# One load for the eight block numbers of a half step, in a graph and attention kernel

## The chip, the cores and the metric

The kernel runs on one core of one Trainium2 chip. The metric is the device time of one execution in microseconds (us). The kernel before has a median of 3451.71 us over three runs (3448.81 to 3453.6).

## The reference, cut to what matters

A node matrix x of 6250 rows by 256 goes through three branches. The first is a graph step: `support = xn @ weight`, then one message for each of 200,000 edges, summed by destination.

```python
support = x @ weight
msgs = edge_val[:, None] * support[edge_col]
agg = jax.ops.segment_sum(msgs, edge_row, num_segments=N_NODES)
return jax.nn.relu(agg + bias + x)
```

In the reference's call the rows that are gathered are numbered by dst and the rows that are summed into by src. The second branch is a linear attention layer with eight heads and a feed-forward layer (the mixer). The third, on the sum of the first two, is a mixture of eight experts with the best two chosen for each row. Only the graph step's sum is touched by the change.

## The kernel before

The kernel has three stages. First the edges are sorted by block of 128 summed rows, and `support` is written to memory. Then comes the gather stage. Then the expert stage follows.

In the gather stage the sorted edges lie in NG = 1624 groups of 128, each group for one block only. Eight groups (HALF = 8) are a half step, and there are STEPS_G = 203 half steps, all written out in the program. A group takes four stations:

- POOL (GpSimd) issues one indirect DMA at L766. It fetches 128 rows of `support` into `rows[h]`. There are ROWS = 4 such buffers, so the gather of half step s waits until the products of half step s - 4 are done (semaphore `summed`). POOL can thus be 32 groups ahead and no more.
- ACT builds the matrix `hot` at L1243 from `is_low`, which DVE makes at L1554 (`select`) three half steps ahead.
- PE multiplies `hot` by `rows` at L929 (`sum_half`), two groups to a unit, each unit in its own PSUM bank. A unit waits for its gathers, and for the adds of the same bank in the half step before (semaphore `carried`).
- DVE adds each product to the running sum of its block: R[block] += ps, L1567 in `carry_on`. These adds are called carries here. The block number is in `dest_i` in SBUF, so DVE's sequencer reads it into a register at L1561 (`value_load`), checks its bounds, works out the address and waits for the carry before and, once for each unit, for PE's products.

The order of work on DVE and PE is written out by hand. On DVE a half step s is `select(s + 3)`, `carry_on(s)`, a `convert` of the next window of edge records every eighth half step, and then pieces of the mixer. Until half step 41 these pieces are the keys and values of the attention. From half step BEGIN = 42 they are the groups of four blocks of the mixer, one group every EVERY = 12 half steps (`widen`, `queries`, `weigh_heads`, `layer_norm`, `add_halves`, `finish`). PE has its own pieces in the same half steps (L946 to L1003). So the carries of DVE, the products of PE and the pieces of the mixer wait for each other in one chain, beside POOL's gathers.

When the mixer's last group is done (`ff2_done`), SP loads the first rows and weights of the expert stage (`first_tail_loads`, L574 and L567), while the last gathers run. After the last carry, `finish(FULL, 1)` ends the stage, and SP and POOL wait for `carried` to reach NG.

In the rows, "DVEq" is DVE's sequencer. TENSOR_LOAD is the register load, the FUSED_REGOPS and the SEQ_ASSERT of L1561 are the bounds check of one number, and the FUSED_REGOPS of L1567 is the address, which also carries the wait for the carry before.

Of the kernel before, what the change touches and what calls it, by code (L numbers as in the profile page):

```python
# [13 lines left out]
ds = bass.ds  # L14
# [15 lines left out]
NB = -(-N // P)  # L30
# [28 lines left out]
HALF = 8  # L59
# [117 lines left out]
def program(nc, x, src, dst, edge_weight, gnn_w, gnn_b, Wq, bq, Wk, bk, Wv, bv, Wo, bo,  # L177
# [10 lines left out]
    with ctx:  # L188
# [3 lines left out]
        def alloc(stack, name, shape, dt=F32):  # L192
            return stack.enter_context(nc.sbuf_tensor(name, shape, dt))
# [85 lines left out]
        dest_i = alloc(early, "dest_i", [P, NG], I32)  # L279
# [27 lines left out]
        R = alloc(early, "R", [P, NB + 1, D])  # L307
# [1055 lines left out]
        def _(dve):  # L1363
# [191 lines left out]
                                  in1=t_low[a][:, None, col:col + HALF].to_broadcast([P, P, HALF]), op=ALU.is_equal).then_inc(is_low_done, 1)  # L1555

            def carry_on(s):
                for q in range(UNITS):
                    for t in range(2):
                        g = s * HALF + q * 2 + t  # L1560
                        where = dve.value_load(dest_i[0:1, g:g + 1], min_val=0, max_val=NB)  # L1561
                        there = R[:, ds(where, 1), :].rearrange("p a d -> p (a d)")
                        if g:
                            dve.wait_ge(carried, g)
                        if t == 0:
                            dve.wait_ge(summed, s * UNITS + q + 1)
                        dve.tensor_tensor(out=there, in0=there, in1=ps[q][:, t * D:(t + 1) * D], op=ALU.add).then_inc(carried, 1)  # L1567
# [113 lines left out]
            for s in range(STEPS_G):  # L1681
                if s + AHEAD_LOW < STEPS_G:
                    select(s + AHEAD_LOW)
                carry_on(s)
                if s % WIN == 1 and s // WIN + 1 < NWIN:
                    convert(s // WIN + 1)
# [285 lines left out]
```

## Time and profile before

| | |
|---|---|
| median of three runs | 3451.71 us |
| the profiled execution's own time | 3441.95 us |
| span of its trace | 3440.2 us |
| gather stage, first gather to last carry | 696.1 to 2813.7 us |
| granted clock of TensorE, mean over the span | 0.83 of full speed |

Every time of the rows is from this one execution. Its own time is 1.75 us above its span, and 9.8 us below the median. Busy time alone doesn't say which engine sets the end of a stage: register, branch and semaphore instructions aren't counted as busy, and POOL needs some time after each DMA before it begins the next.

### The profile page before, as it was taken

The page shows a single profiled execution, that of the slowest core. Times are in us where ns is not written, and L with a number is a line of the kernel's source. Part 1 is how long each engine was busy: PE and PEld are TensorE (multiplying, and loading weights), DVE is VectorE, ACT ScalarE, POOL GpSimd, SP SyncE. Part 2 cuts the span into 40 slices and gives each one's busy share as a digit, 9 for nine tenths or more (in the row PEclk, how much of TensorE's full clock was granted, in tenths as well). Part 3 has the DMA queues.
Part 4 walks back from the last instruction along what each step waited for, and adds up shares of the span by engine and source line. Part 5 has one row for each costly group of instructions (what it writes and reads, how often), then busy time and mean ns, then how long its engine had stood idle before and what let it go on. Part 6 is the DMA issues. An engine that isn't in the chain of part 4 may idle for free.

```text
span 3440.2 us, 46797 instructions
## 1 busy us (share of the span) xinstructions
PE 2606.8 (76%) x10870; PEld 1931.2 (56%) x10870; DVE 2346.8 (68%) x5310; ACT 1248.0 (36%) x2681; POOL 2226.2 (65%) x2110
## 2 busy tenths in 40 slices
PE   5888888667877786786786787787688754888886
PEld 2677777545544454564554565555555533776775
DVE  7999999745555656657656656656656657877863
ACT  0111111045444343344344343343344423444532
POOL 2355555577777777777777777777777733554552
PEclk9666666579889888988898998898898965999998
DMA  3111110065453543453554544445444386555445
GB/s 126 39 34 34 34 34 26 12 127 121 119 125 111 118 117 115 124 121 117 123 119 122 118 119 124 119 116 127 115 107 116 111 185 219 132 130 135 104 87 117
DMA packets 418876, 370.29 MB, mean 108 GB/s; under 512 B 248648, under 2 KB 357232, under 8 KB 418256
## 3 DMA queue, kind: packets, MB, share of 16 engines
q0 software_dynamic: 105424, 247.55, 28.0%
q1 hardware_dynamic: 304720, 110.37, 13.6%
q10 hardware_dynamic: 8496, 9.75, 0.8%
q8 instruction: 84, 1.38, 0.2%
q14 instruction: 152, 1.25, 0.1%
HBM read 299.09 MB, written 74.81 MB: 109 GB/s over the span
## 4 chain that ended last, share of the span: by engine, by line
PE 23%; DVE 20%; issue 12%; POOL 9%; DVEq 7%; DMA 6%; SPq 1%; ACT 1%; POOLq 0%; ACTq 0%
POOL rows L766 8%; DVE R L1567 8%; PE ps L929 6%; DVEq L1561 5%; PE ps L1003 5%; PE ps L995 4%; PE ps L1053 3%; DMA total<-y_w,zt 2%; DMA rows<-support,t_dst 2%; DVEq L1567 1%; DMA zt<-routed 1%; PE ps L963 1%; DVE xnT L1627 1%; DVE is_low L1554 1%; DVE stats L1482 1%
## 5 line engine op out<-in xcount | busy, mean ns | idle before, releaser
L766 POOL DMA_INDIRECT rows<-support,t_dst x1624 | 1598.5, 984 | 503.3 <-issue 462.7
L929 PE MATMUL ps<-rows,hot 128*128 128x256 f32 x3248 | 927.5, 435 | 377.9 <-DVE R L1567 259.8
L1567 DVE TENSOR_TENSOR R<-R,ps 128x256 f32 x1624 | 683.2, 421 | 754.3 <-DVE R L1567 474.8
L929 PEld LDWEIGHTS ps<-rows,hot 128*128 128x128 f32 x3248 | 669.8, 217 | 623.7 <-issue 383.4
L1243 ACT ACTIVATE hot<-is_low,t_w 128x128 f32<-128x128 bf16 x1624 | 689.4, 512 | 188.2 <-DVE is_low L1554 149.3
L740 POOL DMA_INDIRECT slots<-rec,st_pos x224 | 323.3, 1443 | 341.5 <-issue 194.9
L873 PE MATMUL ps<-spread,piece 128*104 128x96 bf16 x1568 | 306.2, 372 | 52.0 <-DVE spread L1476 51.8
L873 PEld LDWEIGHTS ps<-spread,piece 128*104 128x104 bf16 x1568 | 301.4, 286 | 63.8 <-DVE spread L1476 34.0
L810 POOL DMA_INDIRECT total<-y_w,zt x105 | 166.5, 1585 | 235.0 <-DMA total<-y_w,zt 177.2
L1053 PE MATMUL ps<-w_all,h_s 128*128 x1260 | 178.1, 291 | 37.2 <-DVE h_s L1894 36.3
L1053 PEld LDWEIGHTS ps<-w_all,h_s 128*128 128x128 f32 x1260 | 161.6, 192 | 63.9 <-issue 61.4
L1053 PE MATMUL ps<-w_all,z_s 128*128 x630 | 180.4, 423 | 10.3 <-issue 9.3
L1003 PE MATMUL ps<-w_sb,uT 128*128 128x256 f32 x784 | 173.3, 379 | 0.0
L995 PE MATMUL ps<-xnT,w_sb 128*128 128x512 f32 (+1 forms) x416 | 173.1, 568 | 0.0
L1003 PEld LDWEIGHTS ps<-w_sb,uT 128*128 128x128 f32 x784 | 149.0, 190 | 20.3
L789 POOL DMA_INDIRECT routed<-zx,pos_r x98 | 102.8, 1049 | 79.4 <-DVE pos_r L1813 50.5
L1554 DVE TENSOR_TENSOR is_low<-iota_x,t_low 128x1024 bf16<-128x1024 bf16 x203 | 137.8, 679 | 11.5 <-ACT hot L1243 10.0
L1341 ACT ACTIVATE h_act<-h_act 128x512 f32<-128x512 f32 x105 | 66.4, 632 | 215.5 <-DVE h_act L1902 215.5
L1053 PEld LDWEIGHTS ps<-w_all,z_s 128*128 128x128 f32 x630 | 115.5, 195 | 43.8 <-issue 23.6
L1160 ACT ACTIVATE xnT<-ps 128x512 f32<-128x512 f32 (+1 forms) x104 | 53.8, 569 | 219.0 <-PE ps L853 219.0
L1169 ACT ACTIVATE rec<-ps 104x384 bf16<-104x384 f32 x56 | 27.5, 491 | 283.4 <-PE ps L873 283.4
L946 PE MATMUL ps<-wkv_sb,xnT 128*128 128x512 f32 x196 | 107.4, 676 | 23.8 <-ACT h L1250 19.0
(261 smaller groups left out, 3350.5 us busy)
## 6 DMA issues: line engine op xcount, KB each, us to landing
rows<-support,t_dst POOLq DMA_INDIRECT x1624, 2.8
zt<-routed SPq DMA_DIRECT2D x105, 134.0 KB, 2.1
xa<-in_x SPq DMA_DIRECT2D x24, 512.0 KB
out<-total SPq DMA_DIRECT2D x1, 6250.0 KB, 21.7
xin<-in_x SPq DMA_DIRECT2D x12, 512.0 KB
support<-sup_sb ACTq DMA_DIRECT2D x12, 512.0 KB
xf<-in_x SPq DMA_DIRECT2D x12, 512.0 KB
xnb<-xb SPq DMA_DIRECT2D x12, 512.0 KB, 3.6
```

Of the source, the lines that this page charges most:

```text
L740: pool.indirect_dma_start(out=slots, out_offset=bass.IndirectOffsetOnAxis(ap=st_pos[k][0:KP, c:c + 1], axis=0), in_=rec[k][0:KP, c, :, :]. ...
L766: pool.indirect_dma_start(out=rows[h][:, j, :], out_offset=None, in_=support, in_offset=bass.IndirectOffsetOnAxis(ap=t_dst[a][:, col:col + ...
L810: pool.indirect_dma_start(out=total, out_offset=bass.IndirectOffsetOnAxis(ap=zt[i % RING][:, TOK:TOK + 1].bitcast(I32), axis=0), in_=y_w[i ...
L873: last = pe.matmul(ps[2 + half][0:KP, o:o + RUN * NF], lhsT=piece[:, j, :, c], rhs=spread[:, j, :, :, c], start=(j == 0), stop=(j == JT - 1))
L929: last = pe.matmul(ps[q][:, t * D:(t + 1) * D], lhsT=hot[o][:, q * 2 + t, :], rhs=rows[h][:, q * 2 + t, :], start=True, stop=True)
L995: last = pe.matmul(ps[4 + f % 2][:, 0:T], lhsT=w1_sb[:, c, f * P:(f + 1) * P], rhs=hT[:, c, 0:T], start=(c == 0), stop=(c == KC - 1))
L1003: last = pe.matmul(ps[6 + j // 2][:, (j % 2) * D:(j % 2 + 1) * D], lhsT=uT[:, f, j * P:(j + 1) * P], rhs=w2_sb[:, f, :], start=(f == 0), s ...
L1053: ins = pe.matmul(to, lhsT=a(s), rhs=b(m), start=(first and n == 0), stop=(last and n == 2))
L1243: last = act.activation(hot[o][:, k, :], is_low[h][:, :, k], ACT.Copy, scale=t_w[a][:, col:col + 1])
L1554: dve.tensor_tensor(out=is_low[h][:, :, :], in0=iota_x[:, :, :], in1=t_low[a][:, None, col:col + HALF].to_broadcast([P, P, HALF]), op=ALU. ...
L1561: where = dve.value_load(dest_i[0:1, g:g + 1], min_val=0, max_val=NB)
L1567: dve.tensor_tensor(out=there, in0=there, in1=ps[q][:, t * D:(t + 1) * D], op=ALU.add).then_inc(carried, 1)
```

## The change

The eight block numbers of a half step are loaded at the head of `carry_on` by one call that covers eight neighbouring columns of `dest_i`, into eight registers of DVE. The bounds given are the same. The adds then take their numbers from these registers. Nothing else is changed: the order of the adds, their waits and the other engines' programs stay.

```diff
             def carry_on(s):
+                _, where = nc.values_load_multi_w_load_instructions(dest_i[0:1, s * HALF:(s + 1) * HALF], [mybir.EngineType.DVE], min_val=0, max_val=NB)
                 for q in range(UNITS):
                     for t in range(2):
                         g = s * HALF + q * 2 + t
-                        where = dve.value_load(dest_i[0:1, g:g + 1], min_val=0, max_val=NB)
-                        there = R[:, ds(where, 1), :].rearrange("p a d -> p (a d)")
+                        there = R[:, ds(where[q * 2 + t], 1), :].rearrange("p a d -> p (a d)")
                         if g:
                             dve.wait_ge(carried, g)
                         if t == 0:
```

## Rows read from the trace of the kernel before

**Rows 1.** The page's part 1: busy us, share of the span, instructions.

```profile
PE 2606.8 (76%) x10870; PEld 1931.2 (56%) x10870; DVE 2346.8 (68%) x5310; ACT 1248.0 (36%) x2681; POOL 2226.2 (65%) x2110
```

**Rows 2.** Waits of POOL over the span: us in total, times, longest us.

```profile
POOL rows L766 <- issue: 462.7, 1519, 0.3
...
POOL rows L766 <- PE ps L929: 36.6, 104, 3.0
```

**Rows 3.** Gathers (L766) by stretch: stretch, its us, POOL busy (count), clock, DMA, GB/s.

```profile
0.00:1248.00 1248.00, 420.67 (x432) 0.74 0.30 77
...
0.00:2250.00 2250.00, 1186.90 (x1206) 0.80 0.38 96
...
0.00:2548.00 2548.00, 1411.10 (x1432) 0.81 0.39 99
...
0.00:2790.00 2790.00, 1595.55 (x1621) 0.82 0.40 101
```

**Rows 4.** Carries (L1567) by the same stretches: DVE busy (count).

```profile
0.00:1248.00 1248.00, 178.23 (x424) 0.74 0.30 77
...
0.00:2250.00 2250.00, 494.49 (x1176) 0.80 0.38 96
...
0.00:2548.00 2548.00, 588.93 (x1400) 0.81 0.39 99
...
0.00:2790.00 2790.00, 676.43 (x1608) 0.82 0.40 101
```

**Rows 5.** Timeline of POOL: start us, us, instruction, idle before it and its releaser.

```profile
2294.77 0.95 POOL L766 DMA_INDIRECT rows<-support,t_dst  x1 [0.84 <-PE ps L929]
...
2548.28 0.96 POOL L766 DMA_INDIRECT rows<-support,t_dst  x1 [3.00 <-PE ps L929]
```

**Rows 6.** Lines L1561, L1567, DVE's sequencer: ns min/median/max, first and last start.

```profile
L1561 DVEq TENSOR_LOAD <-dest_i x1624: 296/300/1521, 716.9 to 2812.6; - x181
L1561 DVEq FUSED_REGOPS  x1624: 190/190/207, 717.5 to 2812.9; - x181
L1561 DVEq SEQ_ASSERT  x1624: 23/23/39, 717.8 to 2813.1; - x181
...
L1567 DVEq FUSED_REGOPS  x1624: 57/57/57, 717.9 to 2813.2; - x181
```

**Rows 7.** Timeline of DVE in the mixer's part of the gather stage.

```profile
2166.41 0.42 DVE L1567 TENSOR_TENSOR R<-R,ps 128x256 f32 x1 [7.22 <-PE ps L929]
...
2178.40 0.97 DVE L1567 TENSOR_TENSOR R<-R,ps 128x256 f32 x2
...
2232.97 0.42 DVE L1567 TENSOR_TENSOR R<-R,ps 128x256 f32 x1
2233.73 0.42 DVE L1567 TENSOR_TENSOR R<-R,ps 128x256 f32 x1 [0.34 <-DVE R L1567]
2234.56 0.42 DVE L1567 TENSOR_TENSOR R<-R,ps 128x256 f32 x1 [0.41 <-DVE R L1567]
```

**Rows 8.** Line L1561, two short stretches: the first register load of two half steps.

```profile
L1561 DVEq TENSOR_LOAD <-dest_i x1: 309/309/309, 2176.6 to 2176.6; - x1
...
L1561 DVEq TENSOR_LOAD <-dest_i x1: 316/316/316, 2232.1 to 2232.1; - x1
```

**Rows 9.** Waits of DVE, then PE, from 2152 to 2280 us, twelve half steps.

```profile
DVE R L1567 <- PE ps L929: 17.2, 14, 7.2
...
PE ps L929 <- DVE R L1567: 18.7, 11, 5.8
```

**Rows 10.** The stage's end: SP's and PE's timelines; DMA issues, whole span, then 2782 to 2808 us.

```profile
2757.54 0.36 SPq L567 DMA_DIRECT2D work<-xnb  x1
...
2808.33 3.58 PE L929 MATMUL ps<-rows,hot 128*128 128x256 f32 x8 [1.26 <-DMA rows<-support,t_dst]
...
rows<-support,t_dst POOLq DMA_INDIRECT x1624, 2.8
...
rows<-support,t_dst POOLq DMA_INDIRECT x10, 16.0
```

## The prediction, made before the change was run

> **What bounds the kernel now.** I read the page first. PE is the busiest engine, DVE and POOL come behind it, and none is near full [rows 1], so busy shares don't name the bound. The gather stage takes 2118 of 3440 us, and the change lies wholly in it, so I asked each engine there what it waits for.
>
> POOL's answer decides. It issues 1624 gathers, and before 1519 of them its idle time is put down to nothing but issue, 462.7 us or 0.30 us each. The other 104 were released by PE, 36.6 us in all; taking 0.30 us off each of those as the same issue time leaves 5.4 us [rows 2]. So POOL stands truly still for about 5 us in the stage and otherwise issues without a pause. Three of those waits stick out; the first is 0.84 us at 2294, the last 3.00 us at 2548 [rows 5].
>
> Next I counted gathers and carries over the same stretches, which shows how far POOL is ahead of DVE. At 1248 us it is 432 - 424 = 8 groups, at 2250 us 1206 - 1176 = 30, at 2548 us 1432 - 1400 = 32, at 2790 us 1621 - 1608 = 13 [rows 3, 4]. The ring of four `rows` buffers allows 32. So the reader should see two chains. POOL needs 1002 / 774 = 1.295 us for a group between 1248 and 2250 us, the chain of PE, DVE and mixer pieces 1002 / 752 = 1.332 us [rows 3, 4]. For the 96 groups of twelve half steps that is 124.3 against 127.9 us. The chain is a little slower, eats the ring's slack for some nine mixer groups, and only then makes POOL wait. POOL sets the stage's length; the chain costs the 5 us at its end.
>
> **The change part by part.** Before, each carry costs DVE's sequencer one load of 0.300 us, a check of 0.190 and 0.023 us, and an address of 0.057 us [rows 6]. That is 0.57 us. Carries of one unit start 0.76 us apart [rows 7]: 2233.73 less 2232.97. So 0.76 - 0.57 = 0.19 us lie between four instructions, 0.047 us each. The first carry of a unit also waits for PE's semaphore; it comes 0.83 us after the one before (2234.56 less 2233.73), 0.07 us more. Eight carries span 4 x 0.76 + 3 x 0.83 = 5.5 us from the first start to the last, plus 0.85 us from the first load at 2232.1 to the first carry at 2232.97 [rows 7, 8].
>
> What sets this pace is the sequencer: a carry itself takes 0.42 us [rows 7], and DVE idles 0.34 to 0.41 us before the next. Where registers and wait were ready, two carries took 0.97 us together [rows 7], that is 0.55 us apart.
>
> - Removed: seven of eight loads per half step, 7 x 0.35 us of sequencer time. The checks stay, one for each number, since the bounds are still given; I see nothing that would merge them into less work.
> - Moved: all eight checks now stand ahead of the first carry. Load 0.30, checks 8 x (0.190 + 0.023) = 1.70, address 0.06, and 18 gaps of 0.047 = 0.85: 2.9 us from the load's start to the first carry, against 0.85 us. Behind it the carries follow at 0.55 us, a span of 7 x 0.55 = 3.9 us instead of 5.5 us. Sequencer-held half steps therefore take 2.9 + 3.9 = 6.8 us instead of 6.35: +0.45 us. The reason is that the seven removed loads and checks used to run partly under the 0.42 us of the carry ahead of them; the moved ones have no carry to hide under.
> - The price of a load of eight registers is not in this trace. From below it is 0.30 us, a load of one. From above it is eight loads, 8 x 0.35 = 2.8 us. I take about 0.3 us. The recorded load is mostly a trip to SBUF and back, since an instruction that stays in the sequencer takes 0.02 to 0.06 us [rows 6], and one instruction makes one trip.
>
> The Trainium skill speaks against the change here. "Perfetto Trace Analysis", section "DVE / Act Engine Instruction", says that the sequencer pushes an engine instruction into a wait queue and is then free to decode the next. By that rule work spread between carries is partly free, work in front of the first is not. The trace agrees: the load of the next number was over before the carry's 0.42 us were. Left to that rule alone, every half step would pay the 0.45 us.
>
> But a half step is not always held by the sequencer. I went through the twelve of one mixer group, 2149 to 2276 us, from the first register load of each to its first carry.
>
> - In four, DVE waits for PE's product, 7.22 us in the longest case [rows 7]; there the 2.9 us are hidden. All gain 1.6 us of span, but PE is then busy with its own mixer work, and only one of the four, at 2166 us, stands ahead of DVE work that PE needs: -1.6 us.
> - In five, the load starts while DVE still works off queued mixer pieces, so the first carry comes 1.8 to 3.8 us after it; 2176.6 to 2178.40 us is the shortest case [rows 7, 8]. Such a half step loses at most 2.9 - 1.8 = 1.1 us and gains 1.4 to 1.6 us of span: -0.3 us at least, -1.4 us at the longest cover, about -3 us for the five.
> - Three are like 2232.1 us, held by the sequencer: +0.45 us each. The last stands before a wait for PE and costs nothing, so +0.9 us.
>
> The sum is -3.7 us a group, 127.9 to about 124.2 us, level with POOL's 124.3. That this is DVE's to give shows in the waits: in those 126 us PE waits 18.7 us for carries, DVE 17.2 us for products [rows 9]. The ring's slack is then no longer eaten, and POOL's waits of 5 us go. POOL's own 0.98 us and 0.30 us per gather are untouched, and they hide all the rest. If that cover were gone the change would be worth 12 x 3.7 = 44 us.
>
> Before half step 42 the chain is faster than POOL, and 0.45 us more for a half step against a slack of 24 groups (32 - 8) delays nothing.
>
> **The end of the stage.** SP's first loads for the expert stage go out at 2757.54 us, when the mixer is done. From then the gathers land late: a median of 16.0 us after issue between 2782 and 2808 us against 2.8 us over the whole span, and the last products start at 2808.33 us, released by a gather's landing [rows 10]. With the chain no longer 13 to 32 groups behind, the mixer ends nearer to POOL's last gathers in order, so the loads begin about 5 us earlier against POOL's count, and four more gathers land in the slow stretch. From 2757.5 to 2808.3 us POOL's pace has room for 51 / 1.295 = 39 gathers, and the landing time grows by 13.2 us, 0.34 us a gather; four more make about +1.5 us. The last four carries lose 0.2 us each where PE doesn't hold them: -0.2 us. Behind the stage all is shifted alike.
>
> **The rivals.**
>
> - The front load is too dear (slower). If the load of eight costs far over 0.3 us, the half steps that are held by the sequencer, and those with a short cover, pay it, about 6.5 in a group. The gain of 3.7 us is gone at 2.9 + 3.7 / 6.5 = 3.5 us ahead of the first carry, a load of 0.87 us. As the ring's slack is used up today, each further us per group counts twelvefold, and +0.6 us a group makes the kernel slower by 7 us. At 0.1 us for each further register the load takes 1.0 us: +0.9 us a group, 11 us, 3463 us. If the call is only eight loads in a row, so that the change doesn't do what it says, the front is 5.2 us: 6.5 x 2.3 - 3.7 = +11 us a group, 130 us, 3580 us. For it speaks that the trace prices no such load; against it, the short times of all that stays in the sequencer.
> - Hidden anyway (same). If what makes POOL wait at 2294 to 2548 us is PE's mixer work and not the carries, the 5 us stay: 3451 us. PE is what released POOL [rows 5], but PE itself waits 18.7 us for carries in a group [rows 9].
> - The slow landings go too (faster). If the earlier expert loads are through before the last gathers, these land 2.8 us after issue instead of 16.0 us: 13 us on top of 5, about 3434 us. Against it: from 2782 to 2808 us the gathers alone were slow, long after the loads went out, and POOL kept adding to them.
>
> **How the numbers follow.** Sum for the forecast: -5.0 + 1.5 - 0.2 = -3.7 us. The profiled execution's own 3441.95 us would be 3438.3 us; the median of the runs lies 9.8 us above it, and from 3451.7 us I get 3448.0 us. A measurement of this kernel can tell about 0.2%, 7 us, from no change.
>
> Chances: forecast, -1 to -7 us, 0.50; hidden 0.13; dear front load 0.21, of it 0.04 for eight separate loads; landings too 0.16. The forecast and the hidden case are "same", with a little of each neighbour, 0.60; the landings and the forecast's far end are faster, 0.20; the dear load is slower, 0.20. The range reaches from near the landings' case, 3436 us, to a load of somewhat over 1 us, 3470 us: beyond lie some 0.08 below and 0.11 above.
>
> **What would show each step.** In the changed kernel 203 register loads stand where 1624 stood, each near 0.3 us, with eight checks behind it before the first address. First carry 2.9 us after a load's start in sequencer-held half steps; carries 0.55 us apart, not 0.76 and 0.83. POOL less than 25 groups ahead at 2250 us, and no wait over 0.3 us. Last gather issued near 2789 us. The prediction is wrong if the load is over 0.9 us, if the carries stay over 0.7 us apart, if checks are merged or dropped (then the chain is faster still, and the time the same, since POOL holds), or if the landings at the end move by over 5 us.

## The result, and the profile after

The changed kernel takes 3440.13 us, the median of seven runs (3437.51 to 3443.41), against 3451.71 us for the kernel before (seven runs, 3445.84 to 3456.54). The ratio is 0.9966, with a 95% interval of 0.9956 to 0.9976: 11.6 us faster. A later comparison on another chip (e5 below) gave 0.9958 [0.9944, 0.9972].

The profiled execution after has an own time of 3443.41 us and a span of 3441.7 us, 1.5 us longer than the span before. So the two first profiles, laid side by side, don't show the gain at all. The reason lies in the two executions: 3441.95 us is below all seven runs of before, and 3443.41 us is the highest of the seven after. In the experiments a second profile of each kernel was taken, with own times of 3449.48 us (e1, before) and 3438.55 us (e5, after). The readings below use both of each.

The sequencer's rows of L1558 after answer to [rows 6]: ns min/median/max.

```profile
L1558 DVEq FUSED_REGOPS  x1624: 183/183/207, 717.8 to 2799.2; - x181
L1558 DVEq SEQ_ASSERT  x1624: 23/23/39, 718.0 to 2799.4; - x181
L1558 DVEq TENSOR_LOAD <-dest_i x203: 593/597/2609, 716.9 to 2796.6; - x102
```

One load of eight takes 0.597 us, where one of one took 0.300 us: it costs about twice one load, not eight times. All 1624 checks are still there.

One half step after, from DVE's timeline, and the load in front of it, from line L1558 in the same stretch. They answer to [rows 7, 8].

```profile
L1558 DVEq TENSOR_LOAD <-dest_i x1: 593/593/593, 2222.5 to 2222.5; - x1
```

```profile
2225.57 4.37 DVE L1567 TENSOR_TENSOR R<-R,ps 128x256 f32 x8 [2.23 <-issue]
```

The first carry comes 2225.57 - 2222.5 = 3.07 us after the load's start. Then eight carries take 4.37 us together, so (4.37 - 0.42) / 7 = 0.564 us from one to the next. "[2.23 <-issue]" is the checks: DVE is idle, and waits for nothing but its own sequencer.

Gathers and carries after, by stretches from the start, answer to [rows 3, 4].

```profile
0.00:1248.00 1248.00, 420.66 (x432) 0.75 0.30 77
0.00:2250.00 2250.00, 1185.56 (x1210) 0.81 0.38 96
0.00:2548.00 2548.00, 1410.05 (x1440) 0.82 0.40 99
```

```profile
0.00:1248.00 1248.00, 178.30 (x424) 0.75 0.30 77
0.00:2250.00 2250.00, 497.83 (x1184) 0.81 0.38 96
0.00:2548.00 2548.00, 591.99 (x1408) 0.82 0.40 99
```

POOL is 8, 26 and 32 groups ahead, against 8, 30 and 32 before. The ring still fills, but later.

POOL's time goes by one row of the page's part 5: gathers' busy time and mean ns, then the idle time in front of them. First the changed kernel, then its second profile (e5), then the second profile of before (e1).

```profile
L766 POOL DMA_INDIRECT rows<-support,t_dst x1624 | 1592.0, 980 | 502.1 <-issue 461.4
```

```profile
L766 POOL DMA_INDIRECT rows<-support,t_dst x1624 | 1592.5, 981 | 498.8 <-issue 463.5
```

```profile
L766 POOL DMA_INDIRECT rows<-support,t_dst x1624 | 1595.2, 982 | 510.5 <-issue 461.0
```

The kernels of e4 and e10 have no POOL wait over 0.3 us and an idle time of 498.4 and 498.7 us in this row; that is the floor of issuing. Above it stand 3.7 and 0.4 us after, but 12.1 us in e1. In the first profile of before it was 503.3 us, 4.9 us above the floor.

The last carry is at 2813.3 and 2818.3 us before (first profile, e1) and at 2806.5 and 2803.3 us after (first profile, e5). The means lie 10.9 us apart, so the gain is made in the gather stage. The last gather starts at 2792.9 and 2796.9 us before and at 2785.0 and 2783.3 us after: by the means 10.75 us earlier. Of that 6.45 us are idle time of POOL, its waits, and 4.6 us are the gathers themselves, which took 1596.85 us in the mean before and 1592.25 us after (the first gather starts 0.5 us later after). That the change makes gathers shorter is not shown: with three buffers (e6, e7 below) they take 1596.2 and 1596.4 us. The four profiled executions are not the medians either: their own times are only 4.7 us apart in the mean, since what follows the gather stage took some 6 us longer in the two of the changed kernel (last part of the section on the prediction).

### The profile page after: what moved, and what is told of

Same layout as the page of the kernel before. It is cut to its first block, busy times and chain, and to the rows that moved or that the text cites. A ratio compares the mean times of both kernels' runs of the same rounds, so it can differ in the third digit from the quotient of the medians.

```text
span 3441.7 us, 45376 instructions
## 1 busy us (share of the span) xinstructions
PE 2577.5 (75%) x10870; PEld 1934.4 (56%) x10870; DVE 2352.2 (68%) x5310; ACT 1247.5 (36%) x2681; POOL 2218.2 (64%) x2110
## 4 chain that ended last, share of the span: by engine, by line
PE 26%; DVE 25%; issue 9%; DVEq 7%; DMA 6%; POOL 4%; ACT 2%; SPq 1%; POOLq 0%; ACTq 0%
DVE R L1567 10%; PE ps L929 9%; DVEq L1558 6%; PE ps L1003 5%; PE ps L995 5%; PE ps L1053 3%; POOL rows L766 3%; DMA total<-y_w,zt 2%; DMA rows<-support,t_dst 2%; DVEq L1567 1%; DVE is_low L1554 1%; DMA zt<-routed 1%; PE ps L963 1%; DVE xnT L1627 1%; PE ps L946 1%
## 5 line engine op out<-in xcount | busy, mean ns | idle before, releaser
L766 POOL DMA_INDIRECT rows<-support,t_dst x1624 | 1592.0, 980 | 502.1 <-issue 461.4
L1567 DVE TENSOR_TENSOR R<-R,ps 128x256 f32 x1624 | 682.8, 420 | 742.7 <-PE ps L929 304.6
L929 PEld LDWEIGHTS ps<-rows,hot 128*128 128x128 f32 x3248 | 687.8, 220 | 619.1 <-issue 309.8
L1003 PEld LDWEIGHTS ps<-w_sb,uT 128*128 128x128 f32 x784 | 150.0, 191 | 20.7
L1554 DVE TENSOR_TENSOR is_low<-iota_x,t_low 128x1024 bf16<-128x1024 bf16 x203 | 137.4, 677 | 11.5 <-ACT hot L1243 10.0
```

Source lines behind the costliest of these rows:

```text
L766: pool.indirect_dma_start(out=rows[h][:, j, :], out_offset=None, in_=support, in_offset=bass.IndirectOffsetOnAxis(ap=t_dst[a][:, col:col + ...
L929: last = pe.matmul(ps[q][:, t * D:(t + 1) * D], lhsT=hot[o][:, q * 2 + t, :], rhs=rows[h][:, q * 2 + t, :], start=True, stop=True)
L1003: last = pe.matmul(ps[6 + j // 2][:, (j % 2) * D:(j % 2 + 1) * D], lhsT=uT[:, f, j * P:(j + 1) * P], rhs=w2_sb[:, f, :], start=(f == 0), s ...
L1554: dve.tensor_tensor(out=is_low[h][:, :, :], in0=iota_x[:, :, :], in1=t_low[a][:, None, col:col + HALF].to_broadcast([P, P, HALF]), op=ALU. ...
```

## The experiments

Each ratio is against the kernel before, run on the same chip. The chip is one for e1 to e4, another for e5 to e8 and a third for e9 to e11. The floor is POOL's idle time of 498.4 us in e4.

**e1, the kernel before again.** No edit.

> The kernel before, once more, with a profile of its own. Theory: the profiled execution of before was a fast one of its kind (3441.95 us against runs of 3445.84 to 3456.54 us); another profile should show the gather stage's last carry again near 2813 us and the rest of the execution longer than its 627 us, by up to 10 us. Rival: the stage itself varies from run to run by several us, in gathers that take longer than 0.957 us and in waits of POOL; then the last carry lies well over 2813 us in this profile. The time itself: 3446 to 3456 us.

3451.0 us against 3451.62 us, ratio 1.0 [0.999, 1.0009]; last carry at 2818.3 us. The rival holds: the stage itself varies. What doesn't vary is the pace of the chain. L1602, the last piece of `widen`, runs once in each mixer group, so the first and the last of its 13 starts span twelve groups. First the profile of before, then e1:

```profile
L1602 DVE TENSOR_TENSOR xb<-xn,row_b x13: 426/1226/1227, 1123.8 to 2646.3; 128x1024 f32<-128x1024 f32 x12, 128x256 f32<-128x256 f32 x1
```

```profile
L1602 DVE TENSOR_TENSOR xb<-xn,row_b x13: 425/1226/1227, 1126.6 to 2650.3; 128x1024 f32<-128x1024 f32 x12, 128x256 f32<-128x256 f32 x1
```

That is 1522.5 / 12 = 126.9 and 1523.7 / 12 = 127.0 us. POOL's waits are 4.9 and 12.1 us in the same two executions. At the same pace of the chain POOL waits more where its own work goes faster: the gathers took 1595.2 us in e1 and 1598.5 us in the first profile. So the 7.2 us more of waits move its last gather by only 4.0 us.

**e5, the changed kernel again.** No edit.

> The changed kernel once more, with a second profile. Theory: the carry chain has a fixed pace (127.2 us for twelve half steps before, in two profiles; 125.8 us changed) and POOL's waits make up the rest, so a second profile shows 125.6 to 126.0 us again, waits of POOL over 0.35 us that sum to less than the 12.0 us of the second profile of before, and the last carry at 2804 to 2809 us. Rival, that the waits are a matter of chance in both kernels: the sum over 8 us or the last carry over 2812 us.

3438.55 us against 3452.32 us, 0.9958 [0.9944, 0.9972]. The waits, 0.4 us, came as the theory has it. The last carry, 2803.3 us, lies 0.7 us below its range, and the pace of the chain below its 125.6 to 126.0 us. The chain, first after, then e5:

```profile
L1602 DVE TENSOR_TENSOR xb<-xn,row_b x13: 425/1225/1226, 1128.7 to 2633.5; 128x1024 f32<-128x1024 f32 x12, 128x256 f32<-128x256 f32 x1
```

```profile
L1602 DVE TENSOR_TENSOR xb<-xn,row_b x13: 426/1225/1227, 1128.9 to 2631.8; 128x1024 f32<-128x1024 f32 x12, 128x256 f32<-128x256 f32 x1
```

125.4 and 125.2 us a group (by single carries I had expected 125.8): 1.6 us less than before. It also shows the loss. The first mixer group starts at 1128.8 us instead of 1125.2 us, by the means of two profiles: 3.6 us lost. Most of it, 2.7 us, is there at the first carry, which starts at 718.0 us in both profiles before and at 720.1 and 721.3 us after. The 42 half steps up to the mixer add about 1 us. Twelve groups win 12 x 1.6 = 19 us.

**e3, eight single loads in front.**

```diff
-                _, where = nc.values_load_multi_w_load_instructions(dest_i[0:1, s * HALF:(s + 1) * HALF], ...)
+                where = [dve.value_load(dest_i[0:1, s * HALF + k:s * HALF + k + 1], min_val=0, max_val=NB) for k in range(HALF)]
```

> As the changed kernel, but eight single loads with their checks stand in front of the first carry. Theory: the front is 5.2 us instead of 3.0 us, the chain takes some 14 us a group more (about 138 to 140 us against POOL's 124), the slack of 24 groups of edges is eaten within two or three mixer groups, and the kernel takes 3550 to 3590 us. Rival, that the gathers hide the chain at any speed near this: within 10 us of the changed kernel.

3709.7 us, ratio 1.0759 [1.074, 1.0778]. So moving the numbers ahead of the carries is by itself a heavy loss, and the single load is what turns it into a gain. The size was missed by over 100 us. POOL's row and the landmark:

```profile
L766 POOL DMA_INDIRECT rows<-support,t_dst x1624 | 1575.7, 970 | 770.3 <-issue 436.4
```

```profile
L1602 DVE TENSOR_TENSOR xb<-xn,row_b x13: 443/1226/1227, 1216.5 to 2887.7; 128x1024 f32<-128x1024 f32 x12, 128x256 f32<-128x256 f32 x1
```

POOL stands still for 770.3 - 498.4 = 272 us. The mixer groups pace at 1671.2 / 12 = 139.3 us, as expected (138 to 140). The front came as expected too, at 5.1 us where DVE has nothing else to do. What the expectation left out is the part before the mixer: the first group starts at 1216.5 us, 88 us later than in the changed kernel. The longer front is paid there as well, and POOL waits for PE there, 10.5 us in the longest case.

**e2, one load, no checks.** The same call with a stated reason to skip the bounds checks.

```diff
-..., [mybir.EngineType.DVE], min_val=0, max_val=NB)
+..., [mybir.EngineType.DVE], min_val=0, max_val=NB, skip_runtime_bounds_check_because="counts of at most NB flags")
```

> The changed kernel without the bounds checks, so that the front is the load of 0.6 us and the first address. Theory that the chain of products and carries only matters by POOL's waits: twelve half steps of the chain fall from 125.8 to about 114 to 118 us, POOL sets the stage alone, its waits of 3.4 us go, and the kernel takes 3435 to 3441 us, hardly less than the changed one. Rival, that the chain sets the stage: it follows the chain, 8 us a group or over 60 us less.

3436.69 us, 0.9963 [0.995, 0.9976], inside the range, and far from the rival's 60 us. POOL's idle time is 498.3 us: no waits. L1602 runs from 1126.4 to 2609.8 us, 123.6 us a group, not 114 to 118. That number was wrongly reasoned: a chain that has caught up with the gathers can't run ahead of them, so it shows POOL's pace and not its own.

**e4, one load, each number checked at its carry.**

```diff
-                _, where = nc.values_load_multi_w_load_instructions(..., min_val=0, max_val=NB)
+                _, where = nc.values_load_multi_w_load_instructions(..., skip_runtime_bounds_check_because="each is checked where it is used")
...
-                        there = R[:, ds(where[q * 2 + t], 1), :].rearrange("p a d -> p (a d)")
+                        block = nc.s_assert_within(where[q * 2 + t], 0, NB)
+                        there = R[:, ds(block, 1), :].rearrange("p a d -> p (a d)")
```

> One load of eight, but each number is checked just before its own carry. Theory: the front falls from 3.0 to about 1.0 us, the carries stay 0.56 us apart because the next check runs under the carry ahead of it, the chain is as fast as without checks to about 2 us a group, POOL never waits, and the kernel takes 3435 to 3441 us. Rival, that a check costs its time wherever it stands: carries 0.8 us apart and the time of the kernel before or more.

3435.46 us, 0.9958 [0.9946, 0.9971]. All checks are still made. DVE's timeline of one half step, and the landmark (L1604 in this kernel):

```profile
2214.05 0.68 DVE L1554 TENSOR_TENSOR is_low<-iota_x,t_low 128x1024 bf16<-128x1024 bf16 x1
2214.65 2.67 DVE L1569 TENSOR_TENSOR R<-R,ps 128x256 f32 x5
```

```profile
L1604 DVE TENSOR_TENSOR xb<-xn,row_b x13: 460/1226/1227, 1123.9 to 2606.5; 128x1024 f32<-128x1024 f32 x12, 128x256 f32<-128x256 f32 x1
```

Five carries take 2.67 us, (2.67 - 0.42) / 4 = 0.563 us apart, with the check of 0.190 and 0.023 us under each of them, and the first follows `is_low` without a gap. So here a check costs nothing under a carry, while the eight in front of the first carry made the front 3 us long. The landmark gives 1482.6 / 12 = 123.6 us a group, which is POOL's pace. Yet it is not by POOL's waits that e4 gains on the changed kernel: its last gather starts at 2784.4 us, as in the changed kernel's two profiles (2785.0 and 2783.3 us), and its last carry at 2800.7 us, against 2806.5 and 2803.3 us. The difference lies between the two, at the end of the stage (see below).

**e10, the load a half step ahead.** As e4, with the load of the next eight numbers issued between the seventh and the eighth carry.

```diff
                         dve.tensor_tensor(out=there, in0=there, in1=ps[q][:, t * D:(t + 1) * D], op=ALU.add).then_inc(carried, 1)
+                        if q == UNITS - 1 and t == 0:
+                            fetch(s + 1)
```

> The kernel of e4, with the load of the next half step's eight numbers issued between the seventh and the eighth carry. Theory: POOL alone sets the stage in e4, without a wait over 0.35 us, so a faster chain buys nothing: last gather's end 2783 to 2788 us and the kernel within 4 us of e4's 3435.5 us, though the first carry comes about 0.5 us after the sequencer is free instead of 1.0 us. Rival, that the chain still counts: 5 us or more less.

3430.41 us (four runs, 3428.76 to 3436.23), 0.9941 [0.9924, 0.9957]. The stage is no shorter: last carry at 2802.6 us, e4 2800.7 us, POOL's idle time 498.7 and 498.4 us. That is the theory's half about the stage. The time is not: it lies 5.1 us under e4's 3435.5 us, outside the theory's 4 us and in the band of the rival. e4 ran on another chip, and the intervals of the two ratios overlap. Whether the 5 us are real, and where they come from if not from the stage, stays open.

**e6 and e7, three of the four buffers**, for the kernel before and the changed one.

```diff
-ROWS = 4
+ROWS = 3
-        rows = [alloc(early, f"rows{h}", [P, HALF, D]) for h in range(ROWS)]
+        rows = [alloc(early, f"rows{h}", [P, HALF, D]) for h in range(4)]
```

> The kernel before with three of the four rows buffers in use, so POOL can be 24 groups of edges ahead, not 32. Theory: the slack of the ring is eaten some three mixer groups earlier, POOL's waits grow from 12 us by 8 x 1.3 = 10 us, and the kernel takes 3458 to 3466 us. Rival, that the ring plays no part: within 3 us of 3451 us.

> The changed kernel with three of the four rows buffers in use. Theory: as for the kernel before with three, some 10 us more than with four, 3447 to 3455 us, and the difference between the two is again 1.4 us of chain for each of the mixer groups, 10 to 17 us. In the first 42 half steps the chain runs 15 to 18 groups of edges behind, under 24, so no wait arises there. Rival, that the changed kernel gains elsewhere than in POOL's waits: it doesn't mind the lost buffer.

3456.08 us, 1.0013 [1.0003, 1.0022], and 3442.79 us, 0.9975 [0.9964, 0.9986]. Both ranges were too high: against the same kernels with four buffers on this chip (3452.32 and 3438.55 us) the smaller ring costs 3.8 and 4.2 us. The kernels stay 13.3 us apart, in the expected 10 to 17 us. POOL's rows, e6 and then e7:

```profile
L766 POOL DMA_INDIRECT rows<-support,t_dst x1624 | 1596.2, 983 | 519.1 <-issue 462.1
```

```profile
L766 POOL DMA_INDIRECT rows<-support,t_dst x1624 | 1596.4, 983 | 500.1 <-issue 458.7
```

Above the floor of 498.4 us these are 20.7 us for the old chain and 1.7 us for the new one. The old chain's waits grew by 8.6 us with the lost buffer, as they should if the chain is what POOL waits for. But the last carry of e6 is at 2824.0 us, only 5.7 us later than in e1, though its last gather starts 10.8 us later (2807.7 us): a smaller ring delays POOL more than the stage's end. In the changed kernel the waits did not grow (1.7 us, against 3.7 and 0.4 us with four buffers), so there the theory failed and the rival, that it doesn't mind the lost buffer, fits the waits. The 4.2 us of time are not explained by them.

These two profiles are the cleanest pair on the cause. The gathers take the same (1596.2 and 1596.4 us), POOL's idle time falls by 19.0 us, the last gather starts 19.6 us earlier (2788.1 us) and the last carry 20.0 us (2804.0 us).

**e8 and e11, no selection.** The instruction of L1554 is left out from the third half step on, in the changed kernel (e8) and in e4's (e11); the sums are not the reference's.

```diff
+                if s >= 2:
+                    dve.sem_inc(is_low_done, 1)
+                    return
                 dve.tensor_tensor(out=is_low[h][:, :, :], in0=iota_x[:, :, :], ...
```

> The changed kernel without DVE's is_low instruction (L1554) from the third half step on; the products then use the first two selections again, so the sums are not the reference's. Theory: gathers over 1 us are those that meet an instruction of DVE with two operands in SBUF, is_low above all. Then their excess over 0.957 us falls from 39 us to under 15 us, and as the chain also loses 0.68 us a half step POOL never waits: last gather's end at 2750 to 2762 us instead of 2786, kernel 3405 to 3418 us. Rival, that the long gathers have nothing to do with DVE: excess near 39 us, only the 3.4 us of waits go.

> The kernel of e4 without DVE's is_low instruction from the third half step on; the products use the first two selections again, so the sums are not the reference's. In e8 the long gathers went from 41 to 24 us of excess but POOL waited 8 us for a chain at the same 125.3 us. Theory: with the chain of e4 the waits go too, POOL is left with 1624 x 1.257 us and the 24 us of excess, the last gather ends at 2760 to 2766 us (e4: 2785 us) and the kernel takes 3410 to 3418 us. Rival: the excess comes back where the chain is fast, or the waits stay; last gather's end over 2770 us.

3424.76 and 3413.68 us. What led to them is a pattern in the profile of before: gathers take 0.95 us, but some take up to twice as long. POOL, then DVE, at such a place:

```profile
1502.55 0.95 POOL L766 DMA_INDIRECT rows<-support,t_dst  x1 [0.30 <-issue]
1503.81 1.59 POOL L766 DMA_INDIRECT rows<-support,t_dst  x1 [0.30 <-issue]
```

```profile
1503.35 1.23 DVE L1602 TENSOR_TENSOR xb<-xn,row_b 128x1024 f32<-128x1024 f32 x1
1504.49 0.68 DVE L1554 TENSOR_TENSOR is_low<-iota_x,t_low 128x1024 bf16<-128x1024 bf16 x1
```

The long gather stretches over two DVE instructions that read two operands from SBUF, and ends 0.2 us behind them. A carry reads one of its operands from PSUM. Counted over the whole of this profile, none of the 845 gathers that meet only carries takes over 0.97 us, nor does any of the 122 that meet no DVE instruction; of the 252 that meet an `is_low`, 100 take over 1 us. In e8 the gathers, without most such instructions beside them, take 18.6 us less than after (the row after stands above):

```profile
L766 POOL DMA_INDIRECT rows<-support,t_dst x1624 | 1573.4, 969 | 506.9 <-issue 458.5
```

In e11 it is 1573.6 us. So the theory has the cause right and the size wrong: the expectation of e8 was a fall of 24 us or more, from 39 to under 15. The Trainium skill, "SBUF — State Buffer", section "Who interferes with whom", has a rule of this kind: DVE and GpSimd share a port pair, and a DVE instruction with two SBUF inputs contends with a GpSimd instruction that reads SBUF. The rows agree, if a gather, whose row numbers `t_dst` lie in SBUF, counts as one that reads it. e8's time missed its range, also because POOL still waits 506.9 - 498.4 = 8.5 us. The landmark, in e8 and then in e11:

```profile
L1605 DVE TENSOR_TENSOR xb<-xn,row_b x13: 426/1226/1227, 1134.1 to 2625.7; 128x1024 f32<-128x1024 f32 x12, 128x256 f32<-128x256 f32 x1
```

```profile
L1607 DVE TENSOR_TENSOR xb<-xn,row_b x13: 424/1225/1227, 1121.6 to 2589.4; 128x1024 f32<-128x1024 f32 x12, 128x256 f32<-128x256 f32 x1
```

In e8 it gives 124.3 us a group. That is only 1.0 us less than after, though DVE had 12 x 0.68 = 8.2 us less to do, and it is slower than the 122.3 us of e11, where POOL doesn't wait. Most of the work left out had run while the sequencer did its checks: DVE's idle time ahead of carries that is put to "issue" grows from 232.6 us after to 331.7 us in e8. In e11, with the fast chain, POOL's idle time is 498.7 us, the last gather starts at 2764.5 us, and the time is in its range.

**e9, one expert's weights later.** As e4, with the second expert's weights (1 MB) loaded behind the last carry.

```diff
-                for p in range(2):
-                    stage_expert(p)
+                stage_expert(0)
...
-            for p in range(2, 4):
+            for p in range(1, 4):
```

> The kernel of e4 (one load, each number checked at its carry), with 1 MB of the early expert weights (the second expert's) loaded behind the last carry instead of under the last gathers. Theory of the prediction: the early loads make the last gathers land late; with a third less data in them the last landing falls from 13 us after its issue (e4) to 8 us or less, and the stage ends some 5 us earlier, while the later weights cost the expert stage nothing or a few us. Rival, that the gathers once piled up stay slow whatever came before: landing 12 to 14 us after issue again, stage's end within 2 us of e4's 2801 us.

3443.53 us, 0.9977 [0.9966, 0.9988], against 0.9958 for e4. DMA issues from 2774 to 2800 us, with the median us from issue to landing, first e4, then e9:

```profile
rows<-support,t_dst POOLq DMA_INDIRECT x10, 12.2
```

```profile
rows<-support,t_dst POOLq DMA_INDIRECT x10, 11.9
```

The rival holds. With 1 MB less in front of them the last gathers land as late as ever, and the last carry stays (2800.5 us, e4 2800.7 us). The time is 8 us over e4's by the medians, which are from two chips; in the profiles what follows the last carry takes 639.5 us, against 635.0 us in e4. Why the last gathers are slow stays open.

## Why the prediction was right and where it failed

The measured 3440.1 us lies in the range around the predicted 3448.0 us, but the likeliest case (no change that can be measured, 0.60) did not come; "faster" had 0.20. The gain of 11.6 us is three times the 3.7 us of the forecast and outside its own band of 1 to 7 us. The range reaches that far down only for the rival of the landings, which did not come, so that the time fell into it is in part luck.

**POOL and the chain.** Right in the mechanism: POOL issues almost without a pause, the chain is slower than POOL in the mixer groups, eats the ring's slack and then makes POOL wait, and the change pays through these waits. e6 and e7 show this best, with 19.0 of 19.6 us; with four buffers the waits are 6.45 of 10.75 us, and the rest is gathers that happened to be shorter or were made so, which is open. e4, e10 and e2 show the floor that is reached when the waits are gone, and e1 and e6 that a smaller ring makes them longer under the old chain.

**The step that failed** is "the chain costs the 5 us at its end", the first term of the sum. It took POOL's waits from one execution. In the second profile of before they are 12.1 us at the same chain pace, 127.0 us a group. The prediction saw that the profiled execution was 9.8 us under the median, and added this to both sides as a constant. e1's own time is 7.5 us longer. Its waits are 7.2 us longer, but its gathers 3.3 us shorter, so 4.0 us stand at the last gather, another 1.0 us at the last carry, and 2.5 us come behind the stage. The term was 5.0 us; by the means of two profiles each the waits fell from 8.5 to 2.05 us, with four buffers. That is nearer to 5.0 us than to 11.6 us: the term was too small, and the sum lacked the 4.6 us of gathers besides. The term of -0.2 us is too small to be seen beside that.

**The front.** Predicted 2.9 us, measured 3.07 us. The load of eight is 0.6 us, not 0.3 us: 0.04 us for each further register. The reason given for 0.3 us, that what stays in the sequencer takes 0.02 to 0.06 us, passed over the check's 0.190 us in the same rows. The checks were a little cheaper, 0.183 instead of 0.190 us for most. The point from which the rival decides had been put at a load of 0.87 us. e3 is that rival in full, and its price, predicted as 3580 us, was 3709.7 us. The prediction said that the half steps before the mixer have slack enough. For the load of 0.6 us that holds: the chain reaches the mixer 3.6 us later, and POOL's waits for PE up to there are all of 0.3 us, as before. For a front of 5 us it doesn't, and those half steps cost 88 us.

**The carries.** 0.55 us apart was predicted, 0.564 us came.

**The chain.** Predicted -3.7 us a group, measured -1.6 us. By the prediction's own count of half steps the dearer front would account for 6.5 x 0.17 = 1.1 us of the 2.1 us between them, an estimate; the rest is open. In POOL's lead it shows as 26 groups at 2250 us; under 25 were foretold, and 30 stood before.

**The end of the stage.** The prediction said that a chain closer to POOL starts the early expert loads about 5 us sooner against POOL's count and makes the last gathers land later, +1.5 us. Neither came. The first of these loads goes out 35.4 us ahead of the last gather's start in both profiles before and 35.5 us in both after. From the last gather's start to the last carry it is 2813.3 - 2792.9 = 20.4 and, in e1, 21.4 us before, 2806.5 - 2785.0 = 21.5 and, in e5, 20.0 us after: no difference shown. In e4 the loads do start sooner, 41.8 us ahead of the last gather, and there the stretch is shorter, 2800.7 - 2784.4 = 16.3 us, not longer. SP's first load, after and then e4:

```profile
2749.54 0.36 SPq L567 DMA_DIRECT2D work<-xnb  x1
```

```profile
2742.66 0.36 SPq L567 DMA_DIRECT2D work<-xnb  x1
```

All profiles line up in this way. Where the loads start 40.8 to 43.4 us ahead (e2, e4, e6, e7, e9, e10, e11) the stretch is 15.7 to 16.9 us; at 30.5 us ahead (e8) it is 21.4 us, at 13.4 us (e3) 35.6 us. e9 shows that 1 MB less to load changes nothing in it. No run moved the start of the loads alone, so that it sets the stretch is not shown. The rival "the slow landings go too" has this direction, but not in the changed kernel.

**Behind the stage** all was to shift alike. From the last carry to the span's end it is 626.9 and 629.4 us before (first profile, e1), and 635.2 and 633.5 us after. With three buffers it is 630.2 us (e6) and 631.3 us (e7). From so few profiles I can't say whether the expert stage is really some 6 us longer in the changed kernel; the medians, 11.6 and 13.8 us apart, leave no room for it. This stays open.

## What to carry to other kernels

Where a fast engine runs ahead of a slower chain through a ring of buffers, its waits in one profile are a remainder of two large times, and a poor measure of what the chain costs; compare the paces of the two (one landmark line, first and last start), and take a second profile when the first one's own time lies outside the runs.

In these runs the sequencer's work cost nothing while its own engine still executed (e4), and its full time where the engine had nothing left to do (e3). One load for many registers saves the loads, but the checks that come with it gather in front of the first use; load once and check each value where it is used (e4). Before pricing a longer front, count it in every part of the program in which it stands, not only in the part that was read closely.

## What the runs showed of the hardware

- A register load of eight neighbouring numbers took 0.597 us, of one 0.300 us (medians).
- With the bounds check of each number (0.190 and 0.023 us) under the carry ahead of it, carries followed each other at 0.563 us (e4), as fast as with all checks done before (0.564 us, after). With load and check of each number between them it was 0.76 to 0.83 us.
- Leaving out 201 vector instructions with two SBUF operands shortened the gathers issued by POOL by 18.6 us in all (1592.0 to 1573.4 us), though the gathers use nothing that these write.
- The same instructions, 0.68 us each, gave DVE's own chain 1.0 us for twelve half steps when they were left out (e8), of 8.2 us.
- The last gathers of the stage landed 12 us after their issue with or without 1 MB of other loads in front of them.
- The 1624 gathers without their waits took 1592.0 to 1598.5 us in the six profiles of the kernel before and the changed one (four and three buffers), 1592.0 and 1596.4 us in two of the changed kernel alone.
